# Attention over three two-bank slots, with one maximum per two first-pass matmuls and two output blocks moved behind the last of them

## What is computed

```python
def attn(x):                        # x: 2 x 1024 x 512, 8 heads of 8 numbers each
    qk = (x @ Wqk_w.T + Wqk_b).reshape(b, n, H, E, 2)
    q, k = qk[..., 0], qk[..., 1]                       # heads first
    v = (x @ Wv_w.T + Wv_b).reshape(b, n, H, E)
    attn = softmax(einsum('bhqd,bhkd->bhqk', q, k)) / sqrt(64)
    out = einsum('bhsl,bhlv->bhsv', attn, v)
    return out.reshape(b, n, 64) @ Wo_w.T + Wo_b
x = layernorm(x + attn(x))
x = layernorm(x + (silu(x @ Wg.T) * (x @ Wu.T)) @ Wd.T)   # 512 -> 1792 -> 512, int4 weights in groups of 128
```

## Time and profile before

| | us |
|---|---|
| Median of 3 runs (545.93 to 548.78) | 548.14 |
| The profiled execution | 548.8 |
| Its span, first to last instruction | 547.0 |
| Loop of attention, from the first exponential to the end of the last | 58.84 to 232.13 |
| Busy in the span: PE, DVE, ACT, POOL | 514.9, 413.1, 411.8, 243.4 |

### The profile page before, as it was taken

One profiled execution on the slowest core, in us unless ns is written; L12 is line 12 of the kernel. 1 busy time (PEld: TensorE's weight loads), 2 busy tenths in 40 slices (PEclk: granted clock), 3 DMA queues, 4 the chain that ended last, 5 costly groups with the idle time before them and its releaser, 6 DMA issues.

```text
span 547.0 us, 8418 instructions
## 1 busy us (share of the span) xinstructions
PE 514.9 (94%) x3144; PEld 201.8 (37%) x3144; DVE 413.1 (76%) x695; ACT 411.8 (75%) x579; POOL 243.4 (44%) x286
## 2 busy tenths in 40 slices
PE   8798889999899998899999999999999999999992
PEld 3222122222232232234444454444454444544441
DVE  3589888989999993067878888766787666876766
ACT  2441678898899999977788868788777888788771
POOL 8030680730663004038566565843327533257332
PEclk9999798999999999999999999999999999999997
DMA  5585793000004000003212031020000200000201
GB/s 182 190 171 102 208 183 139 1 3 2 1 2 79 3 2 2 0 1 38 40 20 46 13 59 20 1 78 0 1 1 1 77 1 0 2 1 1 77 1 77
DMA packets 29113, 24.98 MB, mean 46 GB/s; under 512 B 19088, under 2 KB 21264, under 8 KB 29072
## 3 DMA queue, kind: packets, MB, share of 16 engines
q1 hardware_dynamic: 25648, 18.41, 12.3%
q0 software_dynamic: 3424, 6.03, 6.1%
HBM read 20.40 MB, written 4.19 MB: 45 GB/s over the span
## 4 chain that ended last, share of the span: by engine, by line
PE 82%; ACT 7%; DVE 6%; DMA 2%; issue 1%; POOL 0%; SPq 0%; POOLq 0%; ACTq 0%; DVEq 0%
PE ps L937 17%; PE ps L949 17%; PE ps L966 17%; PE ps L891 11%; PE ps L875 6%; PE ps L809 6%; ACT pbuf L618 4%; DVE mxh L1064 3%; PE ps L747 3%; PE ps L794 1%; PE ps L852 1%; DMA stack<-mrows 1%; PE ps L975 1%; DMA arena<-xT 1%; PE ps L753 1%
## 5 line engine op out<-in xcount | busy, mean ns | idle before, releaser
L1170 DVE TENSOR_SCALAR ps<-ps,ratio 128x512 f32<-128x512 f32 x168 | 121.7, 755 | 86.3 <-PE ps L949 85.5
L1064 DVE TENSOR_REDUCE mxh<-ps 128x1 f32<-128x512 f32 x256 | 159.1, 684 | 16.2 <-PE ps L809 14.8
L618 ACT ACTIVATE pbuf<-ps,gamma 128x1024 f32<-128x1024 f32 x128 | 140.9, 1113 | 21.1 <-PE ps L875 16.9
L693 ACT ACTIVATE ps<-ps,ratio 128x512 f32<-128x512 f32 x168 | 106.1, 657 | 41.0 <-PE ps L937 41.0
L966 PE MATMUL ps<-stack,wd 128*128 128x512 f16 x448 | 129.6, 379 | 0.6 <-POOL stack L545 0.6
L937 PE MATMUL ps<-arena,wg 128*128 128x512 f16 x448 | 115.4, 379 | 0.9 <-ACT pbuf L701 0.8
L949 PE MATMUL ps<-arena,wu 128*128 128x512 f16 x448 | 115.5, 379 | 0.1
L714 ACT ACTIVATE ps<-ps,ratio 128x512 f32<-128x512 f32 x156 | 102.7, 664 | 16.4 <-PE ps L966 16.3
L891 PE MATMUL ps<-pbuf,arena 128*32 128x256 f32 x1024 | 83.6, 399 | 5.6 <-ACT pbuf L618 3.1
L543 POOL CAST stack<-pbuf 128x512 f16<-128x512 f32 x56 | 34.1, 609 | 114.0 <-DVE pbuf L1177 113.9
L545 POOL TENSOR_TENSOR stack<-pbuf,stack 128x512 f16<-128x512 f32 x56 | 64.7, 1155 | 4.6
(11 more groups left out here) (102 smaller groups left out, 373.7 us busy)
## 6 DMA issues: line engine op xcount, KB each, us to landing
arena<-xT SPq DMA_DIRECT2D x16, 256.0 KB, 5.4
x<-x SPq DMA_DIRECT2D x2, 2048.0 KB, 11.0
out<-x SPq DMA_DIRECT2D x3, 1024.0 KB, 4.2
wg<-gq POOLq DMA_DIRECT2D x4, 448.0 KB, 10.5
wu<-uq POOLq DMA_DIRECT2D x4, 448.0 KB, 12.7
wd<-dq POOLq DMA_DIRECT2D x2, 896.0 KB, 12.8
out<-x SPq DMA_DIRECT2D x4, 256.0 KB, 2.5
wqk_s<-wqkT SPq DMA_DIRECT2D x1, 256.0 KB, 2.7
```

The source lines that it names most:

```text
L618: nc.scalar.activation(pbuf[:, pi % 4, :].rearrange("p (a n) -> p a n", a=2), ps[:, at:at + 2, :], ACT.Exp, scale=gamma[:, n // (ALL // B) ...
L693: nc.scalar.activation(gbank[t % 2], gbank[t % 2], ACT.Copy, scale=gr[:, t % G, c:c + 1])\
L1064: nc.vector.tensor_reduce(mxh[:, f % 2, qh, half:half + 1], ring_bank("first", n), AX.X, ALU.max)\
L1170: nc.vector.tensor_scalar(ubank[t % 2], ubank[t % 2], ur[:, t % G, c:c + 1], None, ALU.mult)\
```

## The change

- **Slots.** The ring and the shared banks are gone from the loop (the 46 matmuls ahead of it keep the ring of 4, 5 and 7). Three slots of two banks, 0 and 1, 4 and 5, 2 and 3, are handed out in the order of one list: scores of half-step h, first-pass pair of h, an output if there is one, scores of h + 1. Each use waits until the one three before it in the list has been read. Bank 7 alone takes the turns M, avT and attT.
- **One maximum for two matmuls.** `reduce_two` reads both banks of a first-pass pair in one instruction, 128 x 2 x 512.
- **Order.** `scores(0, 0)` stands ahead of the loop. In half-step h TensorE now does the first-pass pair of h, then scores of h + 1, then turns, then `av` as before.
- **Outputs of blocks 1 and 2** move to steps 54 to 56 and 58 to 60, behind the last first-pass matmul (step 52). VectorE copies them (`att_out`, `wo_out` under `by_dve`), no longer ScalarE. `att` has two buffers for it. POOL adds blocks 1, 2 and 3 after its last `split_max`.

```diff
-        def shared_banks(*use):
-            return 2 * (shared_index[use] % 2)
+        LOOP = (FIRST - AHEAD) // 4
+        ATT_AT = (STEPS + 2, LOOP + 2, LOOP + 6)
+        WO_AT = (STEPS + 3, LOOP + 3, LOOP + 7)
...
+        def in_slots():
+            order = [("scores", 0)]
+            for h in range(2 * ALL):
+                if firsts_at(h):
+                    order.append(("firsts", h))
+                order += output_at(h)
+                if h + 1 < 2 * ALL:
+                    order.append(("scores", h + 1))
+            return order
...
+        def slot_bank(*use):
+            return (0, 4, 2)[slot_index[use] % 3]
...
+        def wait_slot_read(engine, kind, h, *k):
 
             if kind == "scores":
-                engine.wait_ge(s_exp, 2 * n + k + 1)
+                engine.wait_ge(s_exp, h + 1)
+            elif kind == "firsts":
+                engine.wait_ge(s_rr, AHEAD + 2 * h + 2)
             else:
-                engine.wait_ge(s_read, out_count[kind, n, k])
+                wait_turn_read(engine, kind, h, *k)
...
+            def firsts(h):
+
+                i = slot_index["firsts", h]
+                if i >= 3:
+                    wait_slot_read(pe, *slot_order[i - 3])
+                else:
+                    pe.wait_ge(s_rr, AHEAD)
+                at = slot_bank("firsts", h)
+                for j, m in enumerate(firsts_at(h)):
+                    mm = first_pass(m, bank[at + j])
+                mm.then_inc(s_rf, 2)
...
-            for n in range(ALL):
-                for pair in range(2):
-                    scores(n, pair)
-                    for m in firsts_at(n, pair):
-                        ring_use("first", m)
-                    for use in turns_at(n, pair):
-                        turn(*use)
-                    if n:
-                        av(n - 1, pair)
+            scores(0, 0)
+            for h in range(2 * ALL):
+                if firsts_at(h):
+                    firsts(h)
+                for use in output_at(h):
+                    turn(*use)
+                if h + 1 < 2 * ALL:
+                    scores(*divmod(h + 1, 2))
+                for use in turns_at(h):
+                    turn(*use)
+                if h >= 2:
+                    av(h // 2 - 1, h % 2)
...
+            def reduce_two(h):
+
+                n = firsts_at(h)[0]
+                u, g, tt, qt, half, _ = first_unit(n)
+                f, qh, at = NG * u + g, tt * BT + qt, slot_bank("firsts", h)
+                dve.wait_ge(s_rf, full_count(n + 1))
+                nc.vector.tensor_reduce(mxh[:, f % 2, qh:qh + 2 * BT + 1:2 * BT, half], ps[:, at:at + 2, :], AX.X, ALU.max)\
+                  .then_inc(s_rr, 2)
```

More of the change, by code:

```diff
@@ L178, in build @@
         s_read = sem("turn_read_by_act")
+        s_dread = sem("turn_read_by_dve")
         s_norm = sem("attention_normalised")
@@ L213, in build, with fill_bank, full_count, wait_fill_read @@
         block = ctx.enter_context(nc.Block())
-        def firsts_at(n, pair):
-            m = AHEAD + 4 * n + 2 * pair
-            return range(m, min(m + 2, FIRST))
         before = [("first", n) for n in range(AHEAD)]
         before.insert(FG + 6, ("M", 0))
[L221 to L231, removed]
+        fill_index = {use: i for i, use in enumerate(before)}
+        def fill_bank(*use):
+            return bank[RING[fill_index[use] % 3]]
+        def full_count(n):
+            return fill_index["first", n] + 1 if n < AHEAD else n + 2
+        def wait_fill_read(engine, kind, n):
             if kind == "first":
@@ L236, in wait_ring_read, with firsts_at, output_at, turns_at @@
                 engine.wait_ge(s_m0, 1)
-        def turns_at(n, pair):
+        def firsts_at(h):
+            m = AHEAD + 2 * h
+            return range(m, min(m + 2, FIRST))
+        def output_at(h):
+            n, pair = divmod(h, 2)
+            for u, first in enumerate(WO_AT):
+                if pair and n in (first, first + 1):
+                    return [("wo", u, n - first)]
+            return []
+        def turns_at(h):
+            n, pair = divmod(h, 2)
             if pair == 0:
                 return []
+            if n in ATT_AT:
+                return [("attT", ATT_AT.index(n), 0)]
             f, r = divmod(n + 3, KT)
@@ new lines, in build, with by_dve @@
+        slot_order = in_slots()
+        slot_index = {use: i for i, use in enumerate(slot_order)}
+        single = [use for h in range(2 * ALL) for use in turns_at(h)]
+        single_index = {use: i for i, use in enumerate(single)}
+        all_turns = [use for h in range(2 * ALL) for use in output_at(h) + turns_at(h)] + tail
+        turn_count = {use: i + 1 for i, use in enumerate(all_turns)}
+        def by_dve(use):
+            return use[0] in ("attT", "wo") and 0 < use[1] < NB - 1
+        read_by_act = [use for use in all_turns if use[0] != "avT" and not by_dve(use)]
@@ L546, in inner_parts @@
                   .then_inc(s_ml, 1)
-            for t in range(BT):
-                add_attention(NB - 1, t)
+            for u in range(1, NB):
+                for t in range(BT):
+                    add_attention(u, t)
             for p in range(PERIODS):
@@ L612, in exps @@
             def exps(n, pair):
-                pi, at = 2 * n + pair, shared_banks("scores", n, pair)
+                pi, at = 2 * n + pair, slot_bank("scores", 2 * n + pair)
                 act.wait_ge(s_scf, pi + 1)
@@ L682, in _ @@
                         av_out(n // KT - 1)
-                    for use in turns_at(n, pair):
+                    for use in output_at(2 * n + pair) + turns_at(2 * n + pair):
                         turn_out(*use)
@@ L808, in first_pass @@
                 rows = slice(ROWS * jj, ROWS * (jj + 1))
-                nc.tensor.matmul(ring_bank("first", n), qs[b][rows, k, t, qt * P:(qt + 1) * P],
-                                 ks[b][rows, t, half * TB:(half + 1) * TB], start=True, stop=True).then_inc(s_rf, 1)
+                return nc.tensor.matmul(dst, qs[b][rows, k, t, qt * P:(qt + 1) * P],
+                                        ks[b][rows, t, half * TB:(half + 1) * TB], start=True, stop=True)
             def turn_maxima(f, dst):
@@ L989, in _ @@
             pe.wait_ge(s_gu, 16 * 2 * C)
-            wait_ring_read(pe, "first", FIRST - 1)
+            pe.wait_ge(s_rr, FIRST)
+            pe.wait_ge(s_dread, len(read_by_dve))
+            wait_turn_read(pe, *single[-1])
             for p in range(PERIODS):
```

140 lines of the change are left out of this document (76 added, 64 removed).

## The result

The changed kernel takes **560.85 us** (median of 4 runs, 560.64 at the least), the kernel before 547.53 beside it. The ratio is 1.0235, with a 95% interval of 1.0195 to 1.0276: slower, by 2.35%. The forecast was slower, at 557 with a range of 547 to 562.

What follows compares the result with a forecast made beforehand. VectorE was taken to bound the rhythm before, a circle of waits after. Rhythm + 8.9, turns - 1.3, outputs - 3.7, last stretch + 2.6 and start + 2.5 summed to + 9.0: 557 us, range 547 to 562.

Steps and rivals of the forecast that it cites:

- The step on the rhythm: In the loop, waits from reduction over scores, av and first-pass pair close a circle: 1.295 us a half-step against 1.195.
- The rival in which VectorE is the bound and grouping saves: In the loop, grouping saves every second reduction's start-up: half-step 1.14 us, kernel 538 us; chance 0.12.
- The clock rival: More TensorE pauses in the new circle bring stretches at half clock: kernel 562 to 570 us; chance 0.05.
- The rhythm's term: Half-steps 16 to 104, 89 with first-pass work, each 0.10 us longer: + 8.9 us, bounds + 5.8 and + 16.
- The outputs leaving the loop: Outputs of blocks 1 and 2 leave the loop, saving 1.8 us each: - 3.7 us.
- The last stretch: Exponentials 106 to 127: moved output turns cost 2.0 us, scale ratios ahead of group 6's division 0.6: + 2.6 us.
- Turns of a group: Group turns in the loop: 1.0 us over the rhythm left of 1.25, five times: - 1.3 us.
- The start: Half-steps 0 to 15: slower rhythm, later first av, maxima's rows wanted sooner: + 2.5 us, bounds 0 and + 5.

Runs made afterwards that it cites:

- e3: e1 with av and the turns ahead of the next half-step's scores instead of behind them; 552.24 us, ratio 1.0066 to the kernel before.
- e1: The changed kernel with the first-pass pair and its reduction counting up by 1 instead of 2; 558.77 us, ratio 1.0175 to the kernel before.
- e2: e1 with each pair reduced by two reductions of 512 again, one per bank; 559.2 us, ratio 1.0185 to the kernel before.
- e6: e9 with the moved turns using the ring's banks, free behind the first pass, instead of shared slots; 545.51 us, ratio 0.9957 to the kernel before.
- e4: The changed kernel with outputs of blocks 1 and 2 back inside the loop, at steps 34 to 36 and 50 to 52; 560.93 us, ratio 1.0219.
- e5: The kernel before with the moved outputs alone (VectorE copies, later POOL adds, doubled att), banks still shared; 551.54 us, ratio 1.0059.
- e9: e5 with the scale ratios at step 61; 549.20 us, ratio 1.0011 to the kernel before.
- e7: e1 with the scale ratios at step 61 instead of 56; 556.77 us, ratio 1.0155 to the kernel before.

## Why the prediction was right, and where it was short

**The mechanism was right.** The step on the rhythm named a circle of waits from a reduction's end over scores, `av` and the first-pass pair to the next reduction but one. The chain of the changed kernel shows these pieces in this order, and e3, which takes `av` and the turns out of the circle of e1, gives back 6.5 us. e2 rules out the long reduction as such. The Trainium skill (Perfetto Trace Analysis, Optimizing Scalar/DVE Operations) says that breaking up instructions may let work complete sooner where VectorE or ScalarE isn't saturated but causes bubbles on other engines. In e2 the reduction broken up did not let TensorE go sooner (2.67 us for two half-steps against 2.604), and there the slot comes free with the second half only; no run frees the first bank by itself. The rival in which VectorE is the bound and grouping saves fell with both. The clock rival did not come: the mean granted clock is 0.987 after and 0.985 before.

**The rhythm's term was too small: + 8.9 us forecast, 89 x (1.338 - 1.195) = 12.7 measured.** Of the circle's parts, 0.06, 0.32, 0.57 and the reduction (1.22 forecast, 1.225 measured) were right, the last with some luck: from its own rows, 0.69 + 512 x 0.00109, it comes to 1.25. The hand-over from the pair's start to the reduction's was taken as 0.42 from the earlier trace rows and is 0.50 (167.05, in the timeline, to 167.55). In e1 it is 0.43 (166.07 to 166.50), so 0.07 was the separate wait. (The chain counts the pieces from the end of the work before, so there the pair begins at 167.11 and the scores take 0.38.) The sum comes to 0.05 + 0.31 + 0.58 + 0.50 + 1.23 = 2.67. I had read in the order that the reduction waits for its semaphore before and after, and not asked whether the wait rides on the instruction or stands in front of it.

**The outputs leaving the loop: - 3.7 forecast, - 4.2 to - 4.7 measured.** In the kernel before block 1's outputs cost what the earlier trace rows say, 1.8 us (22.21 to 20.37 for exponentials 64 to 80, before and e6), but block 2's cost 2.35 (14.86 to 12.51 for 96 to 106); in the slots, from e4 to the changed kernel, the two are 2.3 and 2.4. The whole stretch differs by more in some pairs: by 5.1 from before to e6, of which 0.96 us lie in exponentials 16 to 32, where nothing was moved (21.25 to 20.29). From 82 to 92 us the granted clock is 0.83 in the kernel before and in e5, whose stretches differ by 4.1, and 1.00 in e6 and e9. Just ahead TensorE waits for the maxima's rows in all of them, 2.50 us in the kernel before and 1.73 in e6; but the changed kernel has 0.83, too, behind a wait of 1.67, so what decides the clock there these rows do not show.

**The last stretch: + 2.6 forecast, + 2.6 measured, for partly wrong reasons.** The moved turns cost 4.5 there (e4), of which 1.5 are the ratios ahead of the division (e7), forecast at 0.6, and 3.0 the turns in the slots, forecast at 2.0; the order gave back 2.0, forecast at nothing. That the sum came out is luck. The 2.0 were left out because 1.08 us was read as ScalarE's own pace, where it was that of the order: in the changed order an exponential follows the last in 1.01. The ratios took longer, too. VectorE's rows of the changed kernel and POOL's beside them:

```profile
226.14 0.32 DVE L1182 TENSOR_TENSOR small<-scales 128x168 f32<-128x168 f32 x1
226.49 1.25 DVE L1184 TENSOR_SCALAR small<-small 128x168 f32<-128x168 f32 x1
227.78 1.29 DVE L1186 TENSOR_TENSOR scales<-small,scales 128x168 f32<-128x168 f32 x1
```

```profile
223.63 2.49 POOL L549 TENSOR_TENSOR x<-wob,x 128x512 f32<-128x512 f32 x2 [6.84 <-DVE wob L1208]
226.36 2.51 POOL L549 TENSOR_TENSOR x<-wob,x 128x512 f32<-128x512 f32 x2 [0.23 <-DVE wob L1208]
```

The second and third step took 1.25 and 1.29 us; the same lines took 0.25 and 0.33 in the kernel before (248 and 334 ns by its lines view). They lie beside POOL's adds from 226.36 to 228.87, and the first step, begun in the gap of POOL before 226.36, kept its 0.32. e4 is the test, for there the adds come later. Its second, third and last two steps, and POOL's adds:

```profile
221.19 0.25 DVE L1183 TENSOR_SCALAR small<-small 128x168 f32<-128x168 f32 x1
221.47 0.33 DVE L1185 TENSOR_TENSOR scales<-small,scales 128x168 f32<-128x168 f32 x1
...
223.07 1.62 DVE L1192 TENSOR_TENSOR ratio<-scales,small 128x84 f32<-128x84 f32 x2
```

```profile
222.11 4.96 POOL L549 TENSOR_TENSOR x<-wob,x 128x512 f32<-128x512 f32 x4
```

Steps two and three, ahead of the adds, are short again, and the last two, which now lie beside them, take 1.62 us (1.63 in the kernel before), where they take 0.37 in the changed kernel, behind its adds. So what stretches a step is an add beside it (the reciprocal between them takes 1.20 with or without one). The Trainium skill has a rule that fits (SBUF — State Buffer, SBUF: two separate sides): VectorE and GpSimd share a pair of ports, which one instruction holds to its end while the other blocks, if VectorE's instruction runs in a mode that takes both ports or reads two SBUF inputs beside a GpSimd instruction that reads SBUF. The traces agree for the third step and the last two, which read two SBUF inputs: 1.29 us is about the length of one add, 1.25. Which mode the second step ran in no trace here shows.

**Turns of a group: - 1.3 forecast, - 0.7 to - 1.2 measured.** This is what is left of 16 to 106 after the two terms above, 7.3 - 12.7 + 4.7 or + 4.2. A plain group keeps 22.47 - 16 x 1.338 = 1.1 us over the rhythm (exponentials 64 to 80 of the changed kernel) where it had 1.25; 1.0 was forecast. **The start: + 2.5 forecast, + 1.8 measured.** TensorE waited there for the maxima's rows as before (1.67 us beside 2.50).

## What to carry to other kernels

When buffers are handed out in turn from one list, write down for each use what it waits for and follow that back to itself: the sum of a closed walk divided by the rounds it spans is a floor on the rhythm, whatever the engines' busy shares say. Fewer and longer instructions are worth what they save the engine from start to start, and here that was nothing (1.225 us against two at 0.60). Move work that nobody waits for (`av` here) out from between the wait and the next producer, and look again where the circle is gone: the order that cost 6 us against e3's in the loop was the faster one behind the first pass. And work moved into a slack stretch should bring its own buffers along: the same move was + 0.1% in shared slots (e9, an interval that holds 0) and - 0.4% in free ones (e6).

## What was not expected of the hardware

A first-pass pair that adds 2 to its semaphore, and a reduction that adds 2, made each reduction a pair of instructions, a wait of 0.02 us and the reduction; with 1 the wait rides on the reduction. It is worth 0.07 us at each hand-over to an idle VectorE, 2 to 3 us of this kernel (e1). A maximum over two banks costs what its elements cost: 1225 ns for 1024 against 684 for 512, 1.06 ns for each added element, and two of 512 in a row follow each other at 0.60 us, so nothing is gained by joining them. A VectorE step on SBUF of 0.25 or 0.33 us took 1.25 or 1.29 beside a POOL add of 1.25.
